# Graph convolution layers: the node-count comparisons read their numbers from PSUM, and the second bias is added in another place

## What is computed

```
msg   = relu(z[src] + edge_attr @ enc_edge_w + enc_edge_b) + 1e-7
m     = msg * t
ex    = exp(m - segment_max(m, dst)[dst])
agg   = segment_sum(msg * ex / segment_sum(ex, dst)[dst], dst)
out   = relu(layernorm((z + agg) @ w1 + b1) * g1 + bb1) @ w2 + b2
h     = h + out            # layers 1 to 3; layer 0 starts h
z     = relu(layernorm(h) * ln_g + ln_b)
```

## Time and profile before

| | |
|---|---|
| median of 3 runs | 4375.87 us (4375.16 to 4376.1) |
| the profiled execution | 4376.27 us |
| its span, first to last instruction | 4374.4 us |
| DVE busy | 2876.2 us (66%) |
| POOL busy | 3117.8 us (71%) |
| PE busy | 2449.6 us (56%) |
| ACT busy | 1756.3 us (40%) |

### The profile page before, as it was taken

How to read it: one execution, slowest core, us unless ns; L and a number is a source line. 1 busy time by engine, 2 the same in 40 slices (tenths; PEclk the granted TensorE clock), 3 DMA queues, 4 the chain that set the end, 5 groups by cost and what they waited for, 6 DMA issues and landing times.

```text
span 4374.4 us, 37023 instructions
## 1 busy us (share of the span) xinstructions
PE 2449.6 (56%) x9731; PEld 1795.5 (41%) x9731; DVE 2876.2 (66%) x3974; ACT 1756.3 (40%) x3407; POOL 3117.8 (71%) x3248
## 2 busy tenths in 40 slices
PE   4566666665455555555455555555555555555554
PEld 3455545554333333333343333333343333333334
DVE  5777777776566666666656666666665666666665
ACT  2444444444334333333333333333333333333334
POOL 3777777777477777777557777777755777777773
PEclk8767677767577776667657666766656676667775
DMA  3444444454233333333223333333322333333332
GB/s 90 133 133 134 139 138 134 133 140 139 86 99 103 108 103 108 104 108 104 94 59 104 108 104 108 103 109 103 108 76 71 108 104 108 104 108 103 108 103 64
DMA packets 307120, 469.62 MB, mean 107 GB/s; under 512 B 169423, under 2 KB 175305, under 8 KB 306892
## 3 DMA queue, kind: packets, MB, share of 16 engines
q1 hardware_dynamic: 200286, 356.83, 23.8%
q0 software_dynamic: 103552, 109.52, 12.4%
q10 hardware_dynamic: 3054, 0.71, 0.1%
HBM read 217.93 MB, written 248.86 MB: 107 GB/s over the span
## 4 chain that ended last, share of the span: by engine, by line
POOL 70%; issue 23%; PE 2%; DVE 2%; DMA 1%; ACT 1%; POOLq 0%; DVEq 0%; ACTq 0%; SPq 0%
POOL zsrc L518 69%; POOL node_sw L529 1%; DMA zsrc<-z_rows,idx_all 1%; PE pT L789 0%; PE pR L886 0%; PE pX L867 0%; PE pX L778 0%; PE pX L711 0%; ACT sq L642 0%; DVE z L1284 0%; DMA node_sw<-sw_rows,row_idx 0%; DMA sw_rows<-sw_out 0%; DMA x_in<-in_x_dram 0%; ACT sw_out L611 0%; DMA z_rows<-z 0%
## 5 line engine op out<-in xcount | busy, mean ns | idle before, releaser
L518 POOL DMA_INDIRECT zsrc<-z_rows,idx_all x3136 | 3019.5, 963 | 1089.0 <-issue 980.1
L778 PE MATMUL pX<-ident,zsrc 128*128 128x128 f32 x2368 | 604.9, 436 | 1296.7 <-DMA zsrc<-z_rows,idx_all 1296.7
L778 PEld LDWEIGHTS pX<-ident,zsrc 128*128 128x128 f32 x2368 | 518.1, 322 | 1595.3 <-DMA zsrc<-z_rows,idx_all 1595.1
L611 ACT ACTIVATE sw_out<-pT 128x512 f32<-128x512 f32 x784 | 424.8, 594 | 1777.5 <-PE pT L789 1773.3
L1108 DVE TENSOR_TENSOR_SCAN S<-decay,S,pX 128x512 f32<-128x512 f32 x296 | 378.6, 1279 | 678.7 <-ACT decay L603 675.0
L789 PE MATMUL pT<-ident,S 128*128 128x128 f32 x1568 | 637.8, 410 | 43.1 <-DVE W L1112 43.1
L789 PE MATMUL pT<-ident,W 128*128 128x128 f32 x1568 | 627.6, 404 | 0.0
L1091 DVE TENSOR_TENSOR_SCAN M<-pR,M,u 128x512 f32<-128x512 f32 x296 | 377.0, 1274 | 286.7 <-ACT u L598 286.7
L596 ACT ACTIVATE r<-pX,edge_b 128x512 f32<-128x512 f32 x296 | 204.8, 692 | 567.0 <-PE pX L778 567.0
L778 PE MATMUL pA<-ident,zsrc 128*128 128x128 f32 x768 | 194.2, 433 | 422.3 <-DMA zsrc<-z_rows,idx_all 422.3
L773 PE MATMUL pX<-attr_pair,edge_w 128*128 128x512 f32 x592 | 416.0, 791 | 12.3 <-ACT attr_pair L590 12.2
(11 more groups left out here) (201 smaller groups left out, 3100.0 us busy)
## 6 DMA issues: line engine op xcount, KB each, us to landing
sw_rows<-sw_out SPq DMA_DIRECT2D x392, 512.0 KB, 2.9
attr_pair<-attr_cols SPq DMA_DIRECT2D x153, 512.0 KB, 4.4
zsrc<-z_rows,idx_all POOLq DMA_INDIRECT x3136, 2.5
attr_in<-in_edge_attr_dram SPq DMA_DIRECT2D x196, 128.0 KB
attr_cols<-attr_pair SPq DMA_DIRECT2D x49, 512.0 KB, 3.2
max_cols<-M SPq DMA_DIRECT2D x49, 256.0 KB, 3.3
z_rows<-z SPq DMA_DIRECT2D x25, 125.0 KB
node_sw<-sw_rows,row_idx POOLq DMA_INDIRECT x100, 2.5
```

Source lines behind the costliest of these rows:

```text
L518: pool.indirect_dma_start(zsrc[c % RING][:, t4, h, :], None, z_rows, bass.IndirectOffsetOnAxis(idx_all[:, h, t4, c:c + 1].bitcast(U32), 0) ...
L611: act.activation(sw_out[c % 2][:, :, 2 * b:2 * b + 2, :, :].rearrange("p h t s c -> p (t s) h c"), pT[b][:, :].rearrange("p (a h c) -> p a ...
L778: last = pe.matmul(messages_bank(c, first_layer)[:, t4:CH:SUB], zsrc[c % RING][:, t4, :, :].rearrange("p h c -> p (h c)"), ident[:, :], st ...
```

## The change

Five edits.

1. The numbers are kept as f32 in one tile `hi_lo` (125 x 2 x 800). The cast into `hi_b` goes away, and `lo` is written as f32.
2. A new ACT instruction per piece, `hot_numbers(n)`, copies the 20 numbers of piece `n` from SBUF into columns 400 and up of bank `pH`, at one of two places. It stands behind `messages(c)`, waits until PE has used piece `n - 1`, and signals `hot_in`.
3. `node_one_hots` waits for `hot_in` and reads the numbers from `pH` (f32, first input); the second input is `count_b` in SBUF (bf16), the outputs are as before.
4. On PE, `count_nodes` moves ahead of `back` in a chunk.
5. The addition of `b2` into `hres` moves from the start of the layer to behind the last chunk's sums.

```
-        hi_f = sb("hi_f", [NP, ECOLS])
-        hi_b = sb("hi_b", [NP, ECOLS], BF16)
-        lo_b = sb("lo_b", [NP, ECOLS], BF16)
+        hi_lo = sb("hi_lo", [NP, 2, ECOLS])
+        hi_f = hi_lo[:, 0, :]
...
+        def hot_at(n):
+            return 400 + (n % 2) * 2 * HB
...
+                def hot_numbers(n):
+                    if n >= 1:
+                        act.wait_ge(hot_used, n)
+                    act.activation(pH[0:NP, hot_at(n):hot_at(n) + 2 * HB].rearrange("p (s c) -> p s c", s=2),
+                                   hi_lo[:, :, n * HB:(n + 1) * HB], ACT.Copy).then_inc(hot_in, 1)
...
                 for c in range(NCH):
                     messages(c)
+                    if first_layer and 0 <= c - HOT_AT < NHB:
+                        hot_numbers(c - HOT_AT)
                     if first_layer and c + 1 < NCH:
                         attr_to_sb(c + 1)
...
                             attr_to_channels(c + 1)
+                        if 0 <= c - 1 - HOT_AT < NHB:
+                            count_nodes(c - 1 - HOT_AT)
                         if c >= 1:
                             back(c - 1)
-                        if 0 <= c - 1 - HOT_AT < NHB:
-                            count_nodes(c - 1 - HOT_AT)
...
-            v.tensor_copy(hi_b[:, :], hi_f[:, :])
-            v.scalar_tensor_tensor(out=lo_b[:, :], in0=hi_f[:, :], scalar=-float(NK), in1=dst_f[:, :], op0=ALU.mult, op1=ALU.add)
+            v.scalar_tensor_tensor(out=hi_lo[:, 1, :], in0=hi_f, scalar=-float(NK), in1=dst_f[:, :], op0=ALU.mult, op1=ALU.add)
...
-                v.tensor_tensor(hres[:, :, :], hres[:, :, :], b2_all[:, one, :].to_broadcast([NP, NK, H]), ALU.add)
...
-                    cols = slice(n * HB, (n + 1) * HB)
-                    v.tensor_tensor(hot_hi[n % 2][:, :, :], count_b[:, None, 0:NP].to_broadcast([NP, HB, NP]),
-                                    hi_b[:, cols][:, :, None].to_broadcast([NP, HB, NP]), ALU.is_equal)
+                    dve.wait_ge(hot_in, n + 1)
+                    hi, lo = pH[0:NP, hot_at(n):hot_at(n) + HB], pH[0:NP, hot_at(n) + HB:hot_at(n) + 2 * HB]
+                    v.tensor_tensor(hot_hi[n % 2][:, :, :], hi[:, :, None].to_broadcast([NP, HB, NP]),
+                                    count_b[:, None, 0:NP].to_broadcast([NP, HB, NP]), ALU.is_equal)
...
+                v.tensor_tensor(hres[:, :, :], hres[:, :, :], b2_all[:, one, :].to_broadcast([NP, NK, H]), ALU.add)
                 last_s = (NCH - 1) % 2
                 dve.wait_ge(sw_done, g0 + (NCH + PRE))
```

More of the change, by code:

```diff
@@ L248, in program @@
         src_in, src_f_ready, idx_tp, idx_ready = (sem(n) for n in ("src_in", "src_f_ready", "idx_tp", "idx_ready"))
-        hot_ready, hot_used, hist_done, cum_step, cum_mm = (sem(n) for n in ("hot_ready", "hot_used", "hist_done", "cum_step", "cum_mm"))
+        hot_in, hot_ready, hot_used, hist_done, cum_step, cum_mm = (sem(n) for n in ("hot_in", "hot_ready", "hot_used", "hist_done", "cum_step", "cum_mm"))
         seam_known, seam_k_known, rows_known = sem("seam_known"), sem("seam_k_known"), sem("rows_known")
@@ L1039, in _ @@
             dve.drain()
-            v.tensor_scalar(hi_f[:, :], dst_f[:, :], 1.0 / NK, -(NK // 2) / NK, ALU.mult, ALU.add)
+            v.tensor_scalar(hi_f, dst_f[:, :], 1.0 / NK, -(NK // 2) / NK, ALU.mult, ALU.add)
             dve.drain()
-            v.tensor_scalar(hi_f[:, :], hi_f[:, :], ROUND, None, ALU.add)
+            v.tensor_scalar(hi_f, hi_f, ROUND, None, ALU.add)
             dve.drain()
-            v.tensor_scalar(hi_f[:, :], hi_f[:, :], -ROUND, None, ALU.add)
+            v.tensor_scalar(hi_f, hi_f, -ROUND, None, ALU.add)
             dve.drain()
-            v.tensor_copy(hi_b[:, :], hi_f[:, :])
-            v.scalar_tensor_tensor(out=lo_b[:, :], in0=hi_f[:, :], scalar=-float(NK), in1=dst_f[:, :], op0=ALU.mult, op1=ALU.add)
+            v.scalar_tensor_tensor(out=hi_lo[:, 1, :], in0=hi_f, scalar=-float(NK), in1=dst_f[:, :], op0=ALU.mult, op1=ALU.add)
             dve.drain()
@@ L1116, in node_one_hots @@
                         dve.wait_ge(hot_used, n - 1)
-                    cols = slice(n * HB, (n + 1) * HB)
-                    v.tensor_tensor(hot_hi[n % 2][:, :, :], count_b[:, None, 0:NP].to_broadcast([NP, HB, NP]),
-                                    hi_b[:, cols][:, :, None].to_broadcast([NP, HB, NP]), ALU.is_equal)
-                    v.tensor_tensor(hot_lo[n % 2][:, :, :], count_b[:, None, 0:NK].to_broadcast([NP, HB, NK]),
-                                    lo_b[:, cols][:, :, None].to_broadcast([NP, HB, NK]), ALU.is_equal).then_inc(hot_ready, 1)
+                    dve.wait_ge(hot_in, n + 1)
+                    hi, lo = pH[0:NP, hot_at(n):hot_at(n) + HB], pH[0:NP, hot_at(n) + HB:hot_at(n) + 2 * HB]
+                    v.tensor_tensor(hot_hi[n % 2][:, :, :], hi[:, :, None].to_broadcast([NP, HB, NP]),
+                                    count_b[:, None, 0:NP].to_broadcast([NP, HB, NP]), ALU.is_equal)
+                    v.tensor_tensor(hot_lo[n % 2][:, :, :], lo[:, :, None].to_broadcast([NP, HB, NK]),
+                                    count_b[:, None, 0:NK].to_broadcast([NP, HB, NK]), ALU.is_equal).then_inc(hot_ready, 1)
                 def node_ends_1():
```

## The result

The changed kernel takes 4318.47 us (median of 4 runs, 4317.04 to 4319.6), the kernel before 4375.51 (4 runs, 4372.27 to 4376.1). The ratio is 0.987, 95% interval 0.9858 to 0.9881: 57 us faster, where 59.3 was forecast. The forecast for the median was 4316.6 us; the measured one is 1.9 us above it, inside the forecast's 4313 to 4321.

What follows compares the result with a forecast made beforehand. POOL's gathers and their issue pauses bound the kernel; 57.4 (one-hots) + 2.3 (bias) - 0.4 (setup) = 59.3 us less, giving a median of 4316.6 us; own range 4313 to 4321, 8 in 10 for 4311 to 4328.

Steps and rivals of the forecast that it cites:

- the 57.4 us: POOL's 643 gathers during layer 0's node count: 57.4 us lost under comparisons with two SBUF inputs, all taken away.
- The rule that spoke against it: Skill's inference that two-SBUF-input comparisons don't block POOL's DMA descriptors; by it the change would leave 4376 us.
- A gather needs about 0.13 us until it wants something that DVE holds.: POOL's gathers: 0.94 - 0.81 = 0.13 us pass, then the gather waits for the DVE instruction's end.
- A PSUM input costs DVE 0.02 us a chunk: DVE's two comparisons: reading the numbers from PSUM adds about 0.01 us per instruction, 0.02 per chunk.
- The bound of twice the time: DVE's comparisons: upper bound for the broadcast read from PSUM, 1.87 us more per chunk.
- the second rival: DVE becomes the limit if the PSUM broadcast costs double: 20 us given back, 4337 us; chance 7%.
- the slower one: Broadcast read from PSUM takes three times the time on DVE: 112 us more, 4488 us; chance 3%.
- ACT's copy costs nothing: ACT's copy of 20 numbers per piece: 0.203 us, ACT doesn't wait for PE, no cost to the kernel.
- the two reserves: ACT's exponentials behind the copy: 0.35 us before the first is late, 1.0 us before DVE wants the second.
- PE's order costs nothing: PE's count products ahead of `back`: `back` ends 0.70 us later, meeting only L611 and its store; no cost.
- The bias: Addition at the start of layers stretches one gather in each of three, 2.3 us in all; all gone when moved.
- The setup, 0.4 us: Before layer 0: without the cast L1047 starts earlier and holds a gather, costing 0.4 us, bounds 0 and 1.

Runs made afterwards that it cites:

- one line undone: Changed kernel, but both comparisons take their numbers (f32) from SBUF again: 4376.87 us beside 4376.06 for the kernel before, ratio 1.0003.
- the same instruction added elsewhere: Changed kernel plus one unused 125 x 1250 comparison per chunk of layers 1 to 3: 4534.14 us with two SBUF inputs, 4321.68 with one.
- the two experiments on the count: Changed kernel with SBUF numbers again for both comparisons, 4376.87 us, or for the long one only, 4377.45 us; kernel before 4376.06.
- the one on the later layers: Changed kernel plus one unused 125 x 1250 comparison with two SBUF inputs in each chunk of layers 1 to 3: 4534.14 us.
- the first run of the experiments: Changed kernel with both comparisons' numbers from SBUF again, on the chip where the kernel before takes 5060 us: 5091.85 us, ratio 1.0063.
- the four kernels that had it: Changed kernel with numbers from SBUF (ratio 1.0063), only the long comparison from PSUM (1.0173), bias moved back (1.0139, 1.0162), or PE's order undone (1.0217), against the kernel before.

## Why the prediction was right, and where not

- *What bounds the kernel, and the 57.4 us.* Right, and shown from both sides: one line undone brings the held gathers and all of the time back (4376.87 us), and the same instruction added elsewhere costs the forecast sum with two SBUF inputs and nothing with one. The rule that spoke against it falls: by the inference in the Trainium skill, "SBUF — State Buffer", section "Who interferes with whom", a `tensor_tensor` would hold no gather; 288 of the 294 added ones did, each that had a gather begin under it.
- *"A gather needs about 0.13 us until it wants something that DVE holds."* Wrong in the detail. By it a gather that begins up to 0.13 us ahead of the DVE instruction would be held too, and it isn't: which of the two begins first decides. In the kernel before, the two experiments on the count where the kernel before takes 4376 us and the one on the later layers, a gather that begins 0.04 us or more behind the long comparison is held, and one that begins 0.03 us behind or earlier is not; in the first run of the experiments the limit lies between 0.04 and 0.07. The held one ends 0.80 to 0.84 us after the instruction's end, as the prediction read it. The sum didn't hang on it.
- *A PSUM input costs DVE 0.02 us a chunk.* The durations (ns, min/median/max) in the changed kernel:

```profile
L1128 DVE TENSOR_TENSOR hot_hi<-pH,count_b x80: 1448/1449/1452, 96.6 to 886.0; 125x1250 bf16<-125x1250 f32 x80
```

```profile
L1130 DVE TENSOR_TENSOR hot_lo<-pH,count_b x80: 406/407/410, 98.0 to 887.4; 125x250 bf16<-125x250 f32 x80
```

  1.449 and 0.407 us, no more than before (1.45 and 0.42). The bound of twice the time, and with it the second rival and the slower one, didn't come true: the broadcast read of PSUM, which no row had shown, costs nothing more.
- *ACT's copy costs nothing.* Right for the time. It takes 0.168 us, 0.203 was taken. Of the two reserves the first, 0.35 us, was gone: with PE at its lower clock `back` ends near +5.7 us from the start of the nodes instead of +4.7, and the first exponential begins at +6.76 instead of +6.27. The second held: the second exponential ends at 487.67, DVE takes its result at 488.34, 0.67 us later, where 1.0 was forecast. I had read PE's durations from one chunk at a mean clock of 0.72, and the reserve should have been worked out at 0.50. The copy itself was not held up: PE was done with the piece at +3.90 (+3.5 was forecast), 0.17 us before the copy began.
- *PE's order costs nothing.* Right for the time: in the stretch of the count, where alone the order differs, POOL waits for nothing but issue and keeps its pace. What the old order would have cost with the copy there wasn't seen on a chip where POOL is the bound.
- *The bias.* Its place at the end is in DVE's idle time, as forecast; behind layer 0's last sum the DVE timeline has

```profile
1053.07 1.83 DVE L1228 TENSOR_TENSOR hres<-hres,b_all 125x1600 f32<-125x1600 f32 x1
1062.77 0.15 DVE L1232 TENSOR_TENSOR seam_m<-M,seam_fall 64x1 f32<-64x1 f32 x1 [7.88 <-DMA seam_sw<-sw_rows]
```

  1.83 us of the 9.55 of the earlier trace rows. The three holds at the layers' starts are gone. That 2.3 us were gained by it is not shown: from layer 1's first gather to layer 2's, from there to layer 3's, and from there to layer 3's first node gather, the distances moved by +0.7, -1.7 and -0.6 us between the two profiles, so differences of 1 us and more are within what layers do by themselves.
- *The setup, 0.4 us.* Right in kind, too small. POOL and DVE before layer 0:

```profile
59.93 1.37 POOL L521 DMA_INDIRECT zsrc<-z_rows,idx_all  x1 [0.30 <-issue]
...
62.85 1.27 POOL L521 DMA_INDIRECT zsrc<-z_rows,idx_all  x1 [0.30 <-issue]
```

```profile
59.49 0.99 DVE L1058 SCALAR_TENSOR_TENSOR hi_lo<-hi_lo,dst_f 125x800 f32<-125x800 f32 x1
...
62.61 0.69 DVE L1070 TENSOR_TENSOR w1b<-w1b,w_mean 65x512 f32<-65x512 f32 x1
```

  The first hold, 0.43 us, is the forecast one. The second, 0.33 us, and two of 0.06 and 0.07 come from L1070, which moved forward with everything behind the cast; each ends 0.80 to 0.82 us after it. In all 0.89 us, inside the bounds of 0 and 1: every instruction behind a removed one has to be laid over POOL's gathers again. The program's very first gather takes 1.40 us before and 1.39 after; what lengthens it isn't known.
- *The sum.* 57.55 + 2.34 - 0.89 = 59.0 us by the measured terms, 59.2 by the spans, 59.3 forecast; the medians differ by 57.0, since the profiled execution of the changed kernel was the fastest of its four (4317.04 against the median's 4318.47) and that of the kernel before lay above its median (4376.27 against 4375.51). That the forecast span came out to 0.1 us is luck: the terms were off by 0.15, 0.04 and 0.5 us.
- *What the prediction didn't see:* that the same kernel can be bound by something else on another chip. Its rivals all asked what else in the kernel could become the bound; none asked what the added wait costs where POOL isn't it.

## What to carry to other kernels

Where POOL issues gathers back to back, look for gathers longer than their minimum and lay DVE's instructions with two SBUF inputs over them: each one that is longer than the pace catches a gather, here for 0.72 us in the mean, and putting either tile into PSUM takes that away. Put there the input that never changes, if there is one; a copy per piece is one more link between three engines, free here while POOL was the bound; where POOL wasn't, the four kernels that had it lost 0.6 to 2.2%. And time such a change on more than one chip before its worth is told.

## What the runs showed of the hardware

- A gather on POOL that begins behind a DVE instruction with two SBUF inputs is held until that ends and then needs 0.80 to 0.84 us of its ordinary 0.94; which of the two began first decides, to within 0.07 us. The node gathers show the same under a short one: in the changed kernel L1268 (`TENSOR_TENSOR`, 125 x 192) ran from 1068.63 to 1068.99, and the gather begun at 1068.74 took 1.06 us, to 1069.80.
- With one input in PSUM the same comparison of 125 x 1250 holds none (294 added ones, 80 in the count) and takes the same 1.45 us.
- It goes the other way too: in the changed kernel small DVE instructions with one SBUF input ran long beside a gather. A `TENSOR_SCALAR` on 128 x 4 elements took 0.41 us at 63.71 (L1068), 0.17 in the kernel before; it ended at 64.12, together with the gather that had begun at 62.85.
- The kernel before took 4376 us in the runs of the result and on one chip of the experiments, and 5047 to 5060 us on two others. There the instructions of POOL, DVE and ACT had their usual durations, but ACT paused again and again, mostly for 5 to 14 us, in part with no engine at work. Each chip was used for one group of runs, so that a trait of the chip and one of the moment aren't told apart.
